# A four-layer graph network on one core: GpSimd's fixed rests between row gathers replaced by waits on the gather three places ahead

## The reference, cut to what matters

```python
h = jnp.maximum(_layernorm(x, axis=-1), 0.0)
x = x + _L0_gnn_ref(...)   # adj @ h, scaled by rows, times W0, relu
x = x + _L1_gnn_ref(...)   # adj @ (gamma * h W1), hyperbolic norms
x = x + _L2_gnn_ref(...)   # see below
x = x + _L3_gnn_ref(...)   # (I + adj) @ h with scales, norms, times W3
```

```python
h = jnp.einsum('ni,oi->no', x, W) + b
_, topk_idx = jax.lax.top_k(adj, top_k)
h_agg = jnp.max(h[topk_idx], axis=1)
```

## Time and profile before

| | us |
|---|---|
| median of 3 runs | 3664.75 (3662.68 to 3672.45) |
| the profiled execution, its own time | 3679.94 |
| its span | 3678.2 |
| PE busy | 3363.6 (91%) |
| DVE busy | 2618.0 (71%) |
| POOL busy | 2596.3 (71%) |
| ACT busy | 1608.0 (44%) |

### The profile page before, as it was taken

The page is one execution under the profiler, slowest core; times in us unless marked ns, Lnnn a source line. Parts: engine busy times, 40 slices in busy tenths (PEclk is TensorE's granted clock), DMA queues, the critical chain, the costliest instruction groups (busy, mean ns, idle before and its releaser), DMA issues.

```text
span 3678.2 us, 76487 instructions
## 1 busy us (share of the span) xinstructions
PE 3363.6 (91%) x29444; PEld 3338.7 (91%) x29444; DVE 2618.0 (71%) x5491; ACT 1608.0 (44%) x3554; POOL 2596.3 (71%) x2448
## 2 busy tenths in 40 slices
PE   6999999999999999999999999951899999999894
PEld 6999999999999999999999999941899999999894
DVE  5688888778888787421058755747788888888767
ACT  5777887787887887322122122221121111212114
POOL 3999998998998998000288777756888888888600
PEclk9999999999999999999999999975999999999997
DMA  6999999999999999788888998951888889789781
GB/s 208 397 394 391 392 381 365 385 383 353 393 387 357 388 391 368 279 296 289 298 312 311 328 325 314 319 189 44 283 291 293 308 298 324 278 302 325 272 295 58
DMA packets 401324, 1155.22 MB, mean 314 GB/s; under 512 B 36717, under 2 KB 56110, under 8 KB 401006
## 3 DMA queue, kind: packets, MB, share of 16 engines
q1 hardware_dynamic: 360096, 1082.21, 79.7%
q0 software_dynamic: 31360, 64.29, 5.7%
q10 hardware_dynamic: 9550, 4.69, 0.4%
HBM read 874.19 MB, written 276.86 MB: 313 GB/s over the span
## 4 chain that ended last, share of the span: by engine, by line
PE 73%; DVE 15%; issue 6%; POOL 3%; ACT 2%; DMA 1%; DVEq 1%; SPq 0%; POOLq 0%; ACTq 0%
PE psU L668 23%; PE psT L752 16%; PE psT L656 11%; PE psT L784 11%; PE psU L752 5%; PE psU L784 4%; DVE agg L1685 3%; DVE HT L1681 2%; POOL D L507 2%; DVE GR L1844 1%; DVE W L1685 1%; DMA adj_turned<-ATS 1%; DVE agg L1690 1%; POOL D L518 0%; POOL D L499 0%
## 5 line engine op out<-in xcount | busy, mean ns | idle before, releaser
L499 POOL TENSOR_TENSOR D<-D,iota 128x512 f32<-128x512 f32 x1024 | 1306.9, 1308 | 111.6 <-ACT D L911 92.8
L668 PE MATMUL psU<-HB,ATS 128*128 128x129 f32 x8192 | 1008.0, 276 | 22.2 <-ACT ATS L904 20.1
L668 PEld LDWEIGHTS psU<-HB,ATS 128*128 128x128 f32 x8192 | 961.8, 193 | 26.5 <-ACT ATS L904 21.4
L784 PE MATMUL psT<-ATS,PIECES 128*128 128x129 f32 x6144 | 800.5, 281 | 149.5 <-ACT ATS L1070 79.4
L784 PEld LDWEIGHTS psT<-ATS,PIECES 128*128 128x128 f32 x6144 | 751.8, 197 | 158.9 <-issue 133.5
L1474 DVE MAX8 D<-D 128x8 f32<-128x512 f32 x1024 | 644.0, 683 | 254.4 <-POOL D L499 247.0
L752 PE MATMUL psT<-GR,PIECES 128*128 128x129 f32 x6144 | 775.9, 275 | 7.4 <-issue 6.9
L507 POOL DMA_INDIRECT D<-h_table,idx_own x624 | 632.5, 1014 | 170.6 <-issue 150.1
L752 PEld LDWEIGHTS psT<-GR,PIECES 128*128 128x128 f32 x6144 | 730.3, 192 | 10.6 <-issue 10.2
L904 ACT ACTIVATE ATS<-psT 128x512 f32<-128x512 f32 x1024 | 556.4, 597 | 288.9 <-PE psT L656 165.3
L911 ACT ACTIVATE D<-PIECES 128x1024 f32<-128x1024 f32 x512 | 544.4, 1063 | 2.2 <-DVE D L1474 2.2
(11 more groups left out here) (410 smaller groups left out, 2896.0 us busy)
## 6 DMA issues: line engine op xcount, KB each, us to landing
PIECES<-adj_turned SPq DMA_DIRECT2D x512, 1024.0 KB
PIECES<-in_adj SPq DMA_DIRECT2D x256, 1024.0 KB
adj_turned<-ATS SPq DMA_DIRECT2D x512, 512.0 KB, 8.2
D<-h_table,idx_own POOLq DMA_INDIRECT x624
h_table<-HB ACTq DMA_DIRECT2D x8, 512.0 KB, 6.5
D<-h_table,idx_pool POOLq DMA_INDIRECT x215
out_x<-X SPq DMA_DIRECT2D x3, 1024.0 KB, 5.1
ATS<-h_table,idx_pool POOLq DMA_INDIRECT x117
```

Source lines behind the costliest of these rows:

```text
L499: pool.tensor_tensor(key, key, iota[:, :], ALU.mult).then_inc(keyed, 1)
L668: last = nc.tensor.matmul(sum4(r), AT[K % NAT][:, b * GROUP + r * P:b * GROUP + (r + 1) * P], HB[:, j, :], start=(j == 0 and r % 2 == 0), ...
L784: last = nc.tensor.matmul(acc(h, r), block_of(slot, b, r), Hc[par][:, jj, :], start=(jj == 0 and opens(r)), stop=(jj == CT - 1 and closes(r)))
```

## The change

All rests go, with their tiles. Instead each gather but the first three of a list waits until the gather three places ahead of it has landed. To tell that apart, each list's semaphore becomes three: gather k counts on semaphore k mod 3. DVE, which waited on one semaphore for a list, waits on three.

```diff
-BURST = 5
+AHEAD = 3
...
-            def rest(so_far, held):
-                pool.wait_ge(rested, so_far + (2 * rests(0, held) + 2))
+            def landed(done, count):
+                pool.wait_ge(done, count)
                 pool.sem_inc(carrier["pool"], 1)
-                pool.tensor_tensor(idle, idle, idle, ALU.add).then_inc(rested, 1)
-                pool.memset(idle_end[:, :], 0).then_inc(rested, 1)
-
-            def own_gathers(ring, rows, index, done, so_far):
+
+            def own_gathers(ring, rows, index, done, per, turn):
                 for k in range(ring.shape[1]):
-                    if so_far is not NO_REST and k % BURST == 0:
-                        rest(so_far, k)
-                    gather(ring[:, k, :], rows, index[:, k:k + 1], done, 16)
+                    lane = k % AHEAD
+                    if k >= AHEAD:
+                        landed(done[lane], turn * (16 * per[lane]) + 16 * (k // AHEAD))
+                    gather(ring[:, k, :], rows, index[:, k:k + 1], done[lane], 16)
...
+                        if at == 0:
+                            held_by = LANES_FO if held == 0 else lanes_of(0, held)
+                            landed(owned[lane], turn * (16 * (per if held else LANES_FO)[lane]) + 16 * held_by[lane])
+                        else:
+                            landed(done[lane], turn * (16 * per[lane]) + 16 * (before + all_of * at // len(mine)))
...
-            own_gathers(late_own, table, idx_own[0], late_gathered, NO_REST)
-            pool_gathers(late_pool, table, idx_pool[0], n, NEAR_CUTS, late_gathered, NO_REST, OWN_N)
+            own_gathers(late_own, table, idx_own[0], late_gathered, LANES_N, 0)
+            pool_gathers(late_pool, table, idx_pool[0], n, NEAR_CUTS, late_gathered, LANES_N, 0, OWN_N, late_gathered)
...
                 if r == 0:
-                    dve.wait_ge(far_pool_gathered[par], 16 * FAR_POOL * ((g + 1) // 2))
+                    for lane in range(AHEAD):
+                        dve.wait_ge(far_pool_gathered[par][lane], 16 * LANES_FP[lane] * ((g + 1) // 2))
```

More of the change, by code:

```diff
@@ L217, in build @@
         extra = slots(0, TOPK)
-        idle = D[:, 70 * P:72 * P].bitcast(bf16)
         pfx = D[:, 71 * P:72 * P].rearrange("p (k f) -> p k f", f=PREFIX)
@@ L353, in build @@
         idx_staged = sem("idx_staged")
-        near_gathered = [sem(f"near_gathered{i}") for i in range(2)]
-        far_own_gathered = [sem(f"far_own_gathered{i}") for i in range(2)]
-        far_pool_gathered = [sem(f"far_pool_gathered{i}") for i in range(2)]
+        near_gathered = [[sem(f"near_gathered{i}_{j}") for j in range(AHEAD)] for i in range(2)]
+        far_own_gathered = [[sem(f"far_own_gathered{i}_{j}") for j in range(AHEAD)] for i in range(2)]
+        far_pool_gathered = [[sem(f"far_pool_gathered{i}_{j}") for j in range(AHEAD)] for i in range(2)]
         far_pool_free = sem("far_pool_free")
-        early_own_gathered = sem("early_own_gathered")
-        early_pool_gathered = sem("early_pool_gathered")
-        late_gathered = sem("late_gathered")
+        early_own_gathered = [sem(f"early_own_gathered{j}") for j in range(AHEAD)]
+        early_pool_gathered = [sem(f"early_pool_gathered{j}") for j in range(AHEAD)]
+        late_gathered = [sem(f"late_gathered{j}") for j in range(AHEAD)]
         pool_kept = sem("pool_kept")
@@ L390, in pause, with lanes_of @@
                 yield
-        FULL_N = 16 * (OWN_N + NEAR_POOL)
+        def lanes_of(first, end):
+            return [len([k for k in range(first, end) if k % AHEAD == lane]) for lane in range(AHEAD)]
+        LANES_N, LANES_FO, LANES_FP = lanes_of(0, OWN_N + NEAR_POOL), lanes_of(0, OWN_F), lanes_of(0, FAR_POOL)
         PIECES_L1 = NSG * NP
@@ L527, in pool_gathers @@
-            def pool_gathers(ring, rows, index, n, cuts, done, so_far, held):
+                    lane = k % AHEAD
+                    if k >= AHEAD:
+                        landed(done[lane], turn * (16 * per[lane]) + 16 * (k // AHEAD))
+                    gather(ring[:, k, :], rows, index[:, k:k + 1], done[lane], 16)
+            def pool_gathers(ring, rows, index, n, cuts, done, per, turn, held, owned):
+                most = ring.shape[1]
                 def leaf(count):
-                    most = ring.shape[1]
@@ L530, in leaf @@
                     for k in range(count):
[L531 to L536, removed]
+                        lane = (held + k) % AHEAD
@@ new lines, in leaf @@
+                        mine = [m for m in range(count) if (held + m) % AHEAD == lane]
+                        all_of = len([m for m in range(most) if (held + m) % AHEAD == lane])
+                        before = len([m for m in range(held) if m % AHEAD == lane])
+                        at = mine.index(k)
+                        if at == 0:
[3 more added lines that the diff above has]
+                            landed(done[lane], turn * (16 * per[lane]) + 16 * (before + all_of * at // len(mine)))
@@ L537, in pool_gathers @@
+                        share = all_of * (at + 1) // len(mine) - all_of * at // len(mine)
+                        gather(ring[:, k, :], rows, index[:, k:k + 1], done[lane], 16 * share)
                 if len(cuts) == 1:
@@ L542, in pool_gathers, with near_gathers @@
                 with pool.Else():
-                    pool_gathers(ring, rows, index, n, cuts[1:], done, so_far, held)
-            def near_gathers(q, n, staged, so_far):
+                    pool_gathers(ring, rows, index, n, cuts[1:], done, per, turn, held, owned)
+            def near_gathers(q, n, staged, turn):
                 par = q % 2
@@ L548, in near_gathers, with far_gathers @@
                 pool.sem_inc(carrier["pool"], 1)
[L549 to L553, removed]
+                own_gathers(near_own[par], near_table, idx_own[par], near_gathered[par], LANES_N, turn)
+                pool_gathers(near_pool[par], near_table, idx_pool[par], n, NEAR_CUTS, near_gathered[par], LANES_N,
+                             turn, OWN_N, near_gathered[par])
+            def far_gathers(g, n, staged, free, turn):
                 par = g % 2
@@ L566, in _ @@
             pool.wait_ge(head_stored, 16)
-            pool.memset(idle, 0).then_inc(rested, 2)
             with pool.Fori(0, (NG - 2) // 2) as i:
@@ L579, in _ @@
             pool.wait_ge(idx_staged, NG)
-            own_gathers(early_own, early_table, idx_own[1], early_own_gathered, NEAR_RESTS)
+            own_gathers(early_own, early_table, idx_own[1], early_own_gathered, LANES_FO, 0)
             pool.wait_ge(far_pool_free, 1)
-            pool_gathers(early_pool, early_table, idx_pool[1], n, FAR_CUTS, early_pool_gathered,
-                         NEAR_RESTS, OWN_F)
+            pool_gathers(early_pool, early_table, idx_pool[1], n, FAR_CUTS, early_pool_gathered, LANES_FP, 0, 0,
+                         early_own_gathered)
             for s in range(LATE, NSG):
@@ L1575, in near_group @@
                 n = dve.value_load(CTL[0:1, 0, g:g + 1], min_val=1, max_val=NEAR_POOL)
[L1576 removed]
+                for lane in range(AHEAD):
+                    dve.wait_ge(near_gathered[par][lane], 16 * LANES_N[lane] * (q // 2 + 1))
                 if q == 0:
@@ L1599, in early_group @@
                 dve.wait_ge(head_stored, 16)
-                dve.wait_ge(early_own_gathered, 16 * OWN_F)
+                for lane in range(AHEAD):
+                    dve.wait_ge(early_own_gathered[lane], 16 * LANES_FO[lane])
                 dve.sem_inc(carrier["dve"], 1)
@@ L1605, in early_group @@
                     link(v.scalar_tensor_tensor(AGG[:, r, :], AGG[:, r, :], OWNM[:, r:r + 1], gmax, ALU.add, ALU.max))
-                dve.wait_ge(early_pool_gathered, 16 * FAR_POOL)
+                for lane in range(AHEAD):
+                    dve.wait_ge(early_pool_gathered[lane], 16 * LANES_FP[lane])
                 dve.sem_inc(carrier["dve"], 1)
@@ L1619, in late_tile @@
                 else:
-                    dve.wait_ge(late_gathered, FULL_N)
+                    for lane in range(AHEAD):
+                        dve.wait_ge(late_gathered[lane], 16 * LANES_N[lane])
                 dve.sem_inc(carrier["dve"], 1)
@@ L1660, in far_own_rows @@
                 if t % TPG == 0:
-                    dve.wait_ge(far_own_gathered[par], 16 * OWN_F * ((g + 1) // 2))
+                    for lane in range(AHEAD):
+                        dve.wait_ge(far_own_gathered[par][lane], 16 * LANES_FO[lane] * ((g + 1) // 2))
                     dve.sem_inc(carrier["dve"], 1)
```

18 lines of the change are left out of this document (7 added, 11 removed).

## The result

The changed kernel takes **3809.88 us** (median of 4 runs, 3805.67 to 3817.33), the kernel before 3666.11 (4 runs, 3662.68 to 3672.45): a ratio of 1.0394, 95% interval 1.038 to 1.0408. That is 3.9% slower, 92 us over the top of the predicted range.

A forecast was written before the change was run, and what follows sets the result against it. In layer 3 PE and DVE bound the chunks, with the gather stream barely ahead. The slower stream's +17 us, less gains from an earlier start, sooner landings and freed DVE, left +9: 3664.75 + 9 = 3674 us, range 3638 to 3718.

The forecast's parts named there:

- The limit: Layer 3's gather stream: 1.602 us per gather just holds the present time, so the new pace against 1.60 decides.
- The rests' hold on DVE: Rests' additions slow DVE's overlapping instructions: 4.4 us and 1.6 us between the layers, 16 us in layer 3's long chunks.
- Rival one: Layer 3 landings under 4.8 us, pace under 1.60, stream never holds: -28 us, 3637 us; chance 27%.
- The landing: Far gathers: three share one landing time, 5.3 us beside loads, 3.4 on an idle queue, giving a pace of 1.65.
- The mix: Landing time in layer 3 weighted by DMA's busy share, 0.83 x 5.3 + 0.17 x 3.4 = 4.98 us.
- two corrections I let cancel: Layer 3 pace: gain from each list's first three gathers not waiting, against loss from uneven landings; net nothing.
- The near lists at 0: Near lists: first comes 4 us later, PE sees next to nothing; the others have one more stage of cover; cost 0.
- Rival two: Layer 3 gathers' packets wait behind SP's loads: landing 5.4 us, pace 1.80 while loads run, 3715 us; chance 22%.
- Rival one's second half: Landing waits never bind at all, PE and DVE then bound the kernel: also 3637 us; chance 3%.

The follow-up runs named there:

- three_sems: Changed kernel with the old rests back (none in the late list), keeping three semaphores per list and DVE's three waits: 3666.34 us, 1.0002 of before.
- rest_each: Changed kernel with one memset ahead of every gather instead of landing waits, none in the late list: 3697.32 us, 1.0093 of before.
- far_waits: Changed kernel with old rests in near and early lists, no pause in the late list, landing waits only in far lists: 3771.18 us, 1.0285 of before.
- long_memset_rest: Changed kernel with the old rests back, each rest's addition replaced by a memset of 1024 one-byte elements: 3633.47 us, 0.9910 of before.
- near_waits: Changed kernel with landing waits only in near and early lists, old rests in far lists, no pause in the late list: 3715.99 us, 1.0125 of before.
- no_pace: Changed kernel with neither landing waits nor rests in any list: 4642.79 us, 1.2609 of before.
- ahead5: Changed kernel with each gather waiting for the fifth ahead of it instead of the third: 4642.63 us, 1.2607 of before.

## Why the prediction was wrong

- **The limit, right.** "The change is decided by its new pace against 1.60" holds: three_sems at 1.60 is at before's time, rest_each at 1.67 is 32 us over it, far_waits at 1.78 is 107 over it (590 x 0.18 = 106). The product agrees almost by itself, since the 590 gathers fill layer 3. The evidence is that far_waits differs from three_sems in nothing but what paces the far lists.
- **The rests' hold on DVE, right.** Rival one summed the gains to 28 us, of which the additions' hold is 22 and the other 6 need the rests gone; long_memset_rest, which frees DVE of the additions, keeps the rests and nearly the pace (a step of 1.49 for 1.51), gains 32. That the sum comes so near is in part luck. In the changed kernel the gain is there (L1671, the same addition, 293 ns) and buried.
- **The landing, the step that failed.** "The mix is 0.83 x 5.3 + 0.17 x 3.4 = 4.98, so a pace of 1.65." (4.98 / 3 is 1.66.) Measured: 5.34 us for three, 1.78. As a mean the mix wasn't too low: over all far gathers of the changed kernel landing and handoff are 3.4 + 1.4 = 4.8 us, and beside loads that have nearly stopped, 2.2 + 1.2 to 1.4 is close to the 3.4 taken for an idle queue. What failed is the sentence behind it, "two corrections I let cancel". They didn't: a late landing holds all behind it, an early one can't be used, and the gathers bunch. The held gathers had a turn of 4.5 + 1.4 = 5.9 us, all others 5.1, the pauses between lists included; together that is 5.34. The unmixed 5.3 from the earlier trace rows would have hit this mean, by luck, for it stood for gathers that are waited for, and those took 5.9. This step is worth 590 x (1.78 - 1.65) = 77 us.
- **The near lists at 0, the second step that failed.** "The other near lists have one more stage of cover." The cover was some 30 us for all of them together, not anew for each: at 1.94 instead of 1.70 us a gather the delays add up to 74 us at the last near gather (it ends at 2450 us against 2376 in three_sems), and the late list starts 41 us later. near_waits: 52 us. The forecast was low for the first near list already: its 28 gathers take 55 us from the first start to the last, against 41 in before, and not 4 more. I had asked only what PE loses, but behind the last near list stands DVE's chain between the layers.
- **Rival two had the mechanism** and nearly the pace, 1.80, and still said 3715, 95 us too little. It let 7.4 of a chunk's 39.6 gathers pass in PE's pauses at 1.34 us. On the mean of layer 3 they don't: 39.6 x 1.78 = 70.5 us a chunk against its 67.8, over 14 chunks 38 us. The rest is the near lists, which it took over from the forecast at 0.
- **Rival one's second half, wrong in a way nobody saw.** "That the waits never bind at all ... ends at the same time", 3637. no_pace, and nearly so ahead5, is that case, at 4643. The prediction took a free stream for harmless. The Trainium skill's figure behind it ("DMA: Bandwidth & Descriptors", "Anatomy of one DMA", an estimated 2.15 us for 64 KB) agrees with no_pace, where the loads have nearly stopped and gathers land in 2.2 us. Beside loads they take 4.5 us when somebody waits for them, with three in flight.

## What to carry to other kernels

A wait for the n-th transfer ahead sets a pace of (landing + handoff) / n, where the landing is that under load and nearer to the late ones than to the mean, and the handoff (1.15 to 1.7 us here) belongs to it. Before replacing a fixed pause by such a wait, compare this pace with the one that the consumer needs; here 5.34 / 3 stood against 1.60. And a pause that seems wasted may protect another engine: take it away alone first, and look at PE's waits for "issue". If a pause is needed, choose the instruction that does the least to others: a memset of nearly the addition's length brought 0.9%, and shorter ones, one every fourth gather, 1.0%.

## What the hardware showed that I had not expected

- An unbroken train of row gathers on GpSimd at 1.25 us each starves TensorE from about the eighth gather on: in the far lists of no_pace 7.9 matmuls per us behind the sixth gather, 6.5 behind the seventh, 1.4 behind the eighth, 0.6 behind the eleventh, mean of 15 trains. Matmuls then start at multiples of 0.70 us, without a semaphore wait in the profile. DVE's and ACT's instructions kept their durations in the same stretches (166 ns for DVE's 128x8 ones). What TensorE lacks there, whether its instructions or something else, stays open. The two DMA queues that the profile calls "instruction" (q8, q14) moved 3 packets in the 559 us of these trains behind the eighth gather, and 48 in the other 1141 us from 2900 to 4600; that may be the cause or only follow from PE standing still, and no run tells the two apart.
- It depends on the mean step: 1.25 us gives 4643 us, 1.40 gives 4362, 1.44 gives 3628. The second comes in trains of five with a pause between them, so an unbroken train of eight isn't needed.
- The handoff from the last packet of a gather to the start of the gather that waited for it is 1.15 us (median) with two in flight, 1.4 with three and 1.7 with four.
- The turn of the gathers that were held, landing and handoff, is 4.6, 5.9 and 6.4 us with two, three and four in flight, beside loads that also differ.
